# The first attention's routing of an eight-batch transformer kernel: nine pieces on VectorE, five roots on GpSimd, later output products

## The chip, the cores and the metric

The kernel runs on one core of one Trainium2 chip. The metric is the device time of one execution in microseconds; three runs of the kernel before gave 683.17, 691.25 and 2517.85, with a median of 691.25. A core has TensorE (PE: matmuls and transposes), VectorE (DVE), ScalarE (ACT), GpSimd (POOL) and SyncE (SP); they run their own instruction streams and wait for each other on semaphores. Sixteen DMA engines move data between HBM and the on-chip memories. TensorE's products land in PSUM, eight banks of 2 KB a partition.

## The reference

The input x has 8 batches of 128 rows by 256 columns, the context as many. Four residual blocks follow each other:

```python
x = x + cross_attention(layernorm(x), ctx)      # 16 heads over the 256 columns, rotary angles
x = x + moe(layernorm(x), 64 experts, top 8)    # softmax over the logits, gated expert MLPs
x = x + attention(layernorm(x), ctx)            # over the 128 rows, one head
x = x + moe(layernorm(x), 16 experts, top 4)

def cross_attention(query, key, value):         # per batch b and head h, d = 8
    scores = einsum('bdhn,bdhm->bhnm', rotary(q), rotary(k)) / sqrt(8)
    out = einsum('bhnm,bdhm->bdhn', softmax(scores), v)
    return einsum('oi,bin->bon', Wm, out) + bm
```

In the first expert block a row's logits, their eight largest and the softmax over them decide to which experts the row goes and with which weights. The change lies in the first block and in this routing, which is computed beside it.

## The kernel before, in words

The program has four phases. `project_phase` (0 to 64 us of the profile) makes queries, keys and values. `attend_phase` (to about 274 us) is the first attention together with the routing of the first expert block; all that changes lies in it. `held_phase` loads each expert's rows from HBM and runs the 64 experts; its first load of routed rows (`load_rows`, SyncE, L1174) waits until every scatter of the routing is done. `second_phase` holds the rest.

In `attend_phase` each engine runs a loop of its own over the same positions `at`. A position is a head: 16 a batch, 128 in all, from -20 (`LEAD`) to a little over 128. What an engine does at which position is written in its loop, and for the routing in a table, `RoutingSteps`: each stage has an offset, and batch b does it at position 16 b + offset. The order inside one position is the order of the loop's lines. Nothing is planned at run time: an engine that waits holds everything behind it.

A head goes through the engines in this way:
- **Maxima.** Twenty positions ahead TensorE makes the head's scores once (`score_for_top`, L926, two matmuls into one of two banks `ps_top`), and VectorE takes each row's maximum (`find_top`, L1021). TensorE may fill a bank only after the maximum of two heads before. After eight heads GpSimd cuts the maxima into three parts (`cut_tops`), TensorE transposes these (`turn_tops`, L934, bank `ps_rows`), ScalarE copies them (`keep_rows`), and SyncE writes them into rows of the queries (`place`), so that the scores come out with the maximum subtracted.
- **Scores and exponentials.** TensorE makes the scores again (`score`, L944, three banks `ps_score`); ScalarE takes the exponential (L1093) into a ring of twelve.
- **Output products.** For each group of four heads TensorE multiplies the exponentials with the values and a column of ones (`weigh`, L956, two halves, at positions 5 and 7 after the group's first head). After two groups, a pair of eight heads, ScalarE copies the pair's output out of PSUM (`keep_out`, L1077, position 8 p + 12 for pair p). For the second pair of batch b that is position 16 b + 20. In batches 0 to 3 ScalarE issues, right before that copy, the loads of the operands of batch b + 4.
- **The way through memory.** SyncE stores the pair to HBM (`store`, L860) and loads a batch's output and its sums packed into 128 partitions (`load_packed`, L869, two halves).

Then comes the routing of a batch, with its offsets in the table before (`AMID`, batches 0 to 4): load 26, share 34 (VectorE: a reciprocal, L1025, and the product with it, L1028), merge 37 (TensorE: Wm, L974), add 38 (VectorE: the residual, L1034, and the row statistics, L523 and L524), scale 39 (VectorE: the reciprocal root, ten short instructions, L532 to L538), norm 42 (ScalarE, L558), turn 46 (TensorE: two transposes), keep 47 (ScalarE, L607), score 51 (TensorE: the logits), choose 52 (VectorE: logits, the eight largest, the mask, L623 to L632), expo 55 (ScalarE), rank 55 (TensorE), places 57 and targets 59 (VectorE: the addresses), weights 62 (ScalarE, L665). From 62 on GpSimd scatters the batch's rows with eight indirect DMAs (L682). The last three batches have tables with smaller offsets.

`lift` is the merge's bias with the mean of the values' bias folded in: one small matmul (`lift_once`) after the inputs of the merge (`op_w`, `op_bias`, `op_gate`) have landed, and one VectorE addition. Right before it, at position -1, TensorE runs 24 warm-up matmuls (L991) whose results nobody reads. The bank `ps_merge` holds merge results, the transposed rows, logits and ranks in turn.

ScalarE also issues DMAs that clear the buffer of the routed rows (`act_empty`, 960 KB each, up to position 40), and ScalarE and SyncE load the first 32 experts' weights into memory that the attention frees: twelve early ones by ScalarE, twenty by SyncE behind its last packed load (L502).

## Time and profile before

| | us |
|---|---|
| runs shown | 683.17, 691.25, 2517.85 |
| their median | 691.25 |
| the profiled execution | 690.62 |
| its span | 688.9 |
| first attention, from the projections' end to its last instruction | 64 to 274 |
| first load of routed rows | 275.03 |

| engine | busy, share of the span |
|---|---|
| TensorE | 482.5 us, 70% |
| VectorE | 384.4 us, 56% |
| GpSimd | 349.4 us, 51% |
| ScalarE | 221.6 us, 32% |

Busy shares are averages over four phases with different limits. For a change inside one phase the timeline of that phase is read: at which time an engine issues the instruction that another waits for, and which wait ends last there. In a timeline row the first number is the start in us from the span's start, the second the duration, and the bracket behind the row the idle time before it with what ended it. TensorE's granted clock is 0.84 on the mean of the whole span; 1.0 is 2.4 GHz and 0.50 is 1.2 GHz.

### The profile page before, as it was taken

How to read it: one execution, taken by the hardware profiler on the slowest of the kernel's cores; microseconds unless marked ns; L12 is line 12 of the kernel's file. 1: busy time of each engine (PE TensorE's matmuls, PEld its weight loads, DVE VectorE, ACT ScalarE, POOL GpSimd, SP SyncE). 2: the span in 40 equal slices, each digit the busy share in tenths (PEclk: the TensorE clock that was granted, in tenths of full speed). 3: DMA queues.
4: the chain of work that ended last, by engine and by line, in shares of the span. 5: the costliest groups of instructions: out<-in, count | busy, mean ns of one | idle time of the engine just before them, and what ended most of it. 6: DMA issues, size and time to landing. Idle time of an engine off the chain costs nothing.

```text
span 688.9 us, 12080 instructions
## 1 busy us (share of the span) xinstructions
PE 482.5 (70%) x3519; PEld 368.4 (53%) x3519; DVE 384.4 (56%) x1235; ACT 221.6 (32%) x578; POOL 349.4 (51%) x476
## 2 busy tenths in 40 slices
PE   0741898888898430699989994157764499999960
PEld 0630344444443210688877783145553499999950
DVE  8981576788786460154444442689955044444426
ACT  0451065555667310333323331134431122222210
POOL 9394221115556673256545537014444867777730
PEclk9985599888899655799999998597765599999985
DMA  5089989746588697789999723961111799999927
GB/s 184 4 203 244 341 291 298 218 94 155 166 238 279 208 402 285 229 270 313 347 298 309 244 95 106 353 273 55 70 69 61 258 388 360 349 353 361 375 100 276
DMA packets 82915, 163.95 MB, mean 238 GB/s; under 512 B 13070, under 2 KB 58142, under 8 KB 81072
## 3 DMA queue, kind: packets, MB, share of 16 engines
q1 hardware_dynamic: 56832, 106.20, 46.3%
q0 software_dynamic: 13968, 32.29, 12.7%
q10 hardware_dynamic: 12064, 24.84, 12.4%
q8 instruction: 24, 0.39, 0.2%
q14 instruction: 27, 0.22, 0.1%
HBM read 104.94 MB, written 66.78 MB: 249 GB/s over the span
## 4 chain that ended last, share of the span: by engine, by line
PE 32%; DMA 13%; DVE 9%; issue 2%; POOL 2%; ACT 1%; SPq 1%; POOLq 0%; DVEq 0%
PE sc_ps L1790 11%; DMA hd_side<-held 6%; PE hd_ps_up L1246 6%; PE sc_ps L1772 5%; DMA rows<-hd_side_out,hd_side_target 3%; PE hd_ps_out L1252 2%; DMA sc_rows<-rows 2%; PE hd_ps_x L1224 2%; PE sc_ps L1780 1%; DVE sc_rows L1879 1%; PE sc_ps L1740 1%; POOL rows L1393 1%; PE sc_ps L1728 1%; DVE sc_n_stats L1473 1%; DMA listed<-sc_empty,sc_index 1%
## 5 line engine op out<-in xcount | busy, mean ns | idle before, releaser
L1021 DVE TENSOR_REDUCE at_top<-at_ps_top 128x2 f32<-128x512 f32 x128 | 83.2, 685 | 46.4 <-PE at_ps_top L926 45.6
L1393 POOL DMA_INDIRECT rows<-hd_out,hd_rows x64 | 62.2, 972 | 59.3 <-DVE hd_out L1344 36.9
L1093 ACT ACTIVATE at_prob<-at_ps_score 128x512 f32<-128x512 f32 x128 | 72.6, 594 | 51.2 <-PE at_ps_score L944 50.6
L926 PE MATMUL at_ps_top<-e_arena 96*128 96x256 bf16 x256 | 57.6, 315 | 37.2 <-PEq L107 21.9
L1246 PE MATMUL hd_ps_up<-hd_x_turned,e_arena 128*128 128x160 f32 x512 | 82.7, 305 | 0.0
L1790 PEld LDWEIGHTS sc_ps<-sc_t_turned,e_w 128*112 128x112 f32 x672 | 80.6, 180 | 2.6
L1790 PE MATMUL sc_ps<-sc_t_turned,e_w 128*112 128x128 f32 x672 | 82.0, 276 | 0.0
L1246 PEld LDWEIGHTS hd_ps_up<-hd_x_turned,e_arena 128*128 128x128 f32 x512 | 76.1, 192 | 8.7 <-issue 6.2
L682 POOL DMA_INDIRECT held<-e_extended,e_address x64 | 62.4, 975 | 28.4 <-issue 17.7
L682 POOL DMA_INDIRECT listed<-e_extended,e_address x32 | 33.6, 1049 | 69.0 <-DVE e_address L674 61.5
L1381 DVE TENSOR_TENSOR hd_inner<-hd_silu,hd_ps_up 128x160 f32<-128x160 f32 x64 | 20.5, 321 | 81.8 <-ACT hd_silu L1331 81.8
L944 PE MATMUL at_ps_score<-e_arena 99*128 99x256 bf16 x256 | 52.1, 293 | 3.2 <-DMA e_arena<-at_top_rows 3.2
L1686 POOL DMA_INDIRECT listed<-sc_empty,sc_index x48 | 46.8, 974 | 14.6 <-issue 12.5
L926 PEld LDWEIGHTS at_ps_top<-e_arena 96*128 96x128 bf16 x256 | 24.0, 107 | 55.3 <-DVE at_top L1021 28.3
L1691 POOL DMA_INDIRECT rows<-sc_out,sc_target x42 | 41.2, 981 | 22.2 <-POOL sc_index L1680 13.1
L956 PE MATMUL at_ps_out<-at_prob,e_arena 128*32 128x256 f32 x512 | 44.6, 423 | 5.4 <-ACT at_out L1077 4.5
L1331 ACT ACTIVATE hd_silu<-hd_ps_up 128x160 f32<-128x160 f32 x64 | 19.5, 304 | 82.4 <-PE hd_ps_up L1246 82.4
L1857 ACT ACTIVATE sc_silu<-sc_ps 112x256 f32<-112x256 f32 x42 | 16.1, 384 | 89.9 <-PE sc_ps L1790 89.9
L1772 PE MATMUL sc_ps<-e_w,sc_inner 112*128 112x256 f32 x168 | 43.3, 380 | 0.1
L899 POOL TENSOR_SCALAR at_top_cut<-at_top 128x16 bf16<-128x16 f32 x16 | 4.0, 252 | 73.0 <-DVE at_top L1021 73.0
L1344 DVE TENSOR_SCALAR hd_out<-hd_ps_out,hd_rows 128x256 f32<-128x256 f32 x64 | 30.9, 484 | 13.7 <-PE hd_ps_out L1252 12.0
L1252 PE MATMUL hd_ps_out<-e_arena,hd_inner 128*128 128x256 f32 x128 | 38.3, 381 | 0.3 <-DVE hd_inner L1381 0.3
(266 smaller groups left out, 911.6 us busy)
## 6 DMA issues: line engine op xcount, KB each, us to landing
e_w<-in_weights SPq DMA_DIRECT2D x42, 704.0 KB, 6.0
e_arena<-in_weights SPq DMA_DIRECT2D x52, 384.0 KB, 11.4
held<-e_empty ACTq DMA_DIRECT2D x16, 960.0 KB, 7.2
hd_rows<-held SPq DMA_DIRECT2D x15, 768.0 KB, 10.5
sc_rows<-rows SPq DMA_DIRECT2D x8, 1024.0 KB, 13.8
sc_tile_rows<-listed SPq DMA_DIRECT2D x42, 144.0 KB
parts<-op_parts SPq DMA_DIRECT2D x8, 576.0 KB, 6.7
e_arena<-in_weights ACTq DMA_DIRECT2D x12, 384.0 KB, 4.0
```

The lines of the kernel that those rows point to most:

```text
L682: self.nc.gpsimd.indirect_dma_start(self.held_dram, to, self.held.extended[:, b, :], None).then_inc(self.held.scattered, 16)
L926: last = nc.tensor.matmul(ps_top[at % TOPS][:, half, :], q_in[n][0:TOP, columns(at, half)], k_in[n][0:TOP, columns(at)], start=True, stop= ...
L944: last = nc.tensor.matmul(ps_score[at % SCORES][:, half, :], k_in[n][0:ROWS, columns(at, half)], q_in[n][0:ROWS, columns(at)], start=True, ...
L956: last = nc.tensor.matmul(ps_out[32 * j:32 * j + VW, g % 2, :], v_in[:, b, half, 4 * g + j, :], prob[(4 * group + j) % RING][:, half, :], ...
L1021: nc.vector.reduce_max(top[:, 2 * h:2 * h + 2], ps_top[at % TOPS][:], AX_X).then_inc(top_found, 1)
L1093: nc.scalar.activation(prob[at % RING][:], ps_score[at % SCORES][:], ACT.Exp, scale=scale).then_inc(prob_ready, 1)
L1246: op = nc.tensor.matmul(ps_up[e % 2][:, part, :], w[:, k, part * P:(part + 1) * P], x_turned[g % 2][:, j, k, :], start=k == 0, stop=k == 1)
L1252: nc.tensor.matmul(ps_out[e % 2][:], inner[e % INNERS][:, 0:P], ring.w[e % ring.SLOTS][:, 2, :], start=True, stop=True).then_inc(down_done, 1)
L1393: nc.gpsimd.indirect_dma_start(rows_out, to, out_ap, None, bounds_check=TOKENS * LAYER0.chosen - 1, oob_is_err=False).then_inc(semaphore, 16)
L1686: nc.gpsimd.indirect_dma_start(listed_dram, to, empty[:], None, bounds_check=E * TOKENS + 2 * U * P - 1, oob_is_err=False).then_inc(cleare ...
L1772: op = nc.tensor.matmul(ps_out[u % 2], inner[u % 2][:, c * P:(c + 1) * P], down_w[u][:, c, :], start=c == 0, stop=c == C - 1)
L1790: op = nc.tensor.matmul(ps_up[u % 2][:, part, c * P:(c + 1) * P], up_w[u][:, k, at:at + W], t_turned[u % 2][:, k, :], start=k == 0, stop=k ...
```

## The change

It moves stages, splits two of them and hands one to another engine; what is computed is the same, but that five roots are computed by a power in place of a first guess and Newton steps.

- Each batch has a table of its own. Of batches 0 to 3: load 25, invert0 30, invert1 31, share 32, merge 35, add 36, stats 37, scale 38, norm 41, turn 44, keep 45, score 49, best 50, mask 51, expo 53, rank 54, places 55, targets 57, weights 60. The scatters of a batch have a table (`SCATTERS`).
- VectorE's reciprocal is in two halves of 128 columns (`invert`), the choice in two pieces (`dve_best`, `dve_mask`), the statistics apart from the addition.
- The roots of batches 0 to 4 run on GpSimd (`pool_scale`, three instructions instead of ten), those of 5 to 7 stay on VectorE.
- The merge results move from the bank `ps_merge` to that of the transposed maxima (`ps_rows_merged`). The merge now waits for ScalarE's copy of these maxima and for the addition before, and some transposes wait for an addition.
- The two halves of the output products stand at 7, 9 and 10, 11 after a pair's first head, where they stood at 5, 7 and 9, 11.
- `lift_once` stands at position -2, ahead of the warm-up, and VectorE's addition at -1.

```diff
 class Rstd:
     def pool_scale(self, pool, link, b):
...
         link(nc.gpsimd.tensor_scalar(full, self.mean_var[:, 1:2], EPS, None, ALU.add))
         link(nc.gpsimd.tensor_tensor(root, full, self.power[:], ALU.pow))
-        for _ in range(NEWTON - 1):
...
 class RoutingSteps:
-    LOAD, SHARE = 26, 34
-    AMID = dict(load=LOAD, share=SHARE, merge=37, add=38, scale=39, norm=42, turn=46, keep=47, score=51, choose=52, expo=55, rank=55,
-                places=57, targets=59, weights=62, scatter=62)
-    LAST_BUT_TWO = dict(AMID, turn=45, keep=46, score=49, choose=49, expo=50, targets=50, rank=50, places=51, weights=51, scatter=53)
-    LAST_TWO = dict(load=LOAD, share=SHARE, merge=35, add=36, scale=37, norm=37, turn=39, keep=39, score=41, choose=41, expo=42, targets=42,
-                    rank=43, places=43, weights=43, scatter=46)
+    AMID = dict(load=25, invert0=30, invert1=31, share=32, merge=35, add=36, stats=37, scale=38, norm=41, turn=44, keep=45, score=49,
+                best=50, mask=51, expo=53, rank=54, places=55, targets=57, weights=60)
+    FOURTH = dict(AMID, score=48, best=49, mask=49, expo=51, rank=51, places=52, targets=53, weights=54)
+    FIFTH = dict(load=25, invert0=30, invert1=30, share=30, merge=34, add=34, stats=34, scale=34, norm=36, turn=39, keep=40, score=43,
+                 best=43, mask=43, expo=45, rank=44, places=45, targets=46, weights=47)
+    SIXTH = dict(load=25, invert0=30, invert1=30, share=30, merge=31, add=32, stats=32, scale=32, norm=33, turn=35, keep=35, score=37,
+                 best=37, mask=37, expo=38, rank=38, places=39, targets=39, weights=40)
+    SEVENTH = dict(load=25, invert0=34, invert1=34, share=34, merge=35, add=36, stats=36, scale=37, norm=37, turn=39, keep=39, score=41,
+                   best=41, mask=41, expo=42, rank=42, places=43, targets=43, weights=43)
+    BATCHES = (AMID, AMID, AMID, AMID, FOURTH, FIFTH, SIXTH, SEVENTH)
+    SCATTERS = ((60, 61, 62, 63, 68, 69, 71, 72),) * 3 + tuple(tuple(range(first, first + 8)) for first in (60, 54, 48, 43, 51))
+    BY_POOL = 5
...
 def attend_phase(...):
-        ps_rows = s.psum("ps_rows", [P, P])
+        ps_rows_merged = s.psum("ps_rows_merged", [P, 2 * D])
+        ps_rows, ps_merged = ps_rows_merged[:, 0:P], ps_rows_merged[:, D:]
         ps_merge = s.psum("ps_merge", [P, 2 * D])
-        ps_merged = ps_merge[:, 0:D]
...
+                b = steps("scale", at)
+                if b is not None and b < steps.BY_POOL:
+                    rstd.pool_scale(pool, link, b)
...
             def turn_tops(hh):
+                if hh == 1:
+                    pe.wait_ge(lift_known, 1)
+                if hh >= 6 and hh % 2 == 0:
+                    pe.wait_ge(x_ready, hh // 2 - 2)
...
             def lift_once():
                 pe.wait_ge(inputs.loaded, 48)
+                pe.wait_ge(rows_kept, 1)
...
             def merge(b):
-                if b >= B - 2:
-                    pe.wait_ge(routing.rank_read, b)
-                elif b >= 1:
-                    pe.wait_ge(routing.logits_read, b)
-                else:
-                    pe.wait_ge(lift_known, 1)
+                pe.wait_ge(rows_kept, min(2 * b + 6, HALVES))
+                if b >= 1:
+                    pe.wait_ge(x_ready, b)
                 pe.wait_ge(divided, b + 1)
...
-                if 4 <= at < B * H + 4 and at % 4 == 1:
-                    weigh(at // 4 - 1, 0)
-                if 4 <= at < B * H + 4 and at % 4 == 3:
-                    weigh(at // 4 - 1, 1)
+                for offset, late_group, half in ((7, 0, 0), (9, 0, 1), (10, 1, 0), (11, 1, 1)):
+                    p, late = divmod(at - offset, HALF)
+                    if late == 0 and 0 <= p < HALVES:
+                        weigh(2 * p + late_group, half)
...
+                if at == -2:
+                    lift_once()
                 if at == -1:
                     for _ in range(WARM_UP):
                         nc.tensor.matmul(ps_score[0][:, 0, :], k_in[0][0:TOP, 0:P], k_in[0][0:TOP, 0:D], start=True, stop=True)
-                    lift_once()
...
                 if b is not None:
-                    if b + 1 < B - 2:
-                        pe.wait_ge(x_ready, b + 2)
                     routing.pe_rank(pe, b)
...
+            def invert(b, half):
+                if half == 0:
+                    dve.wait_ge(packed_loaded[b % 2], 32 * (b // 2 + 1))
+                link.free(nc.vector.reciprocal(share[:, half * P:(half + 1) * P], packed[b % 2][:, 1, half * P:(half + 1) * P]))
+
             def divide(b):
-                dve.wait_ge(packed_loaded[b % 2], 32 * (b // 2 + 1))
-                link(nc.vector.reciprocal(share[:], packed[b % 2][:, 1, :]))
+                dve.wait_ge(link.semaphore, link.count)
...
-                if at == 0:
+                if at == -1:
                     dve.wait_ge(lift_ready, 1)
```

The first place is VectorE's stream over one batch of the middle. `at_top` are the maxima of one head each, `at_share` the reciprocal, `at_heads` the output that the merge takes, `at_r_logits` to `e_mask` the choice of another batch's experts, `x_all` the residual. Before:

```order
L1021 TENSOR_REDUCE at_top<-at_ps_top 128x2 x7
L1025 RECIPROCAL at_share<-at_packed 128x256
L1028 TENSOR_TENSOR at_heads<-at_packed,at_share 128x256
L1021 TENSOR_REDUCE at_top<-at_ps_top 128x2 x2
L623 COPY at_r_logits<-at_ps_merge 128x64
L627 MAX at_r_best<-at_r_logits 128x8
L628 TENSOR_SCALAR at_r_minus_top<-at_r_best 128x1
L631 MATCH_REPLACE at_r_taken<-at_r_best,at_r_logits 128x64
L632 TENSOR_SCALAR e_mask<-at_r_taken 128x64
L1021 TENSOR_REDUCE at_top<-at_ps_top 128x2 x2
L1034 SCALAR_TENSOR_TENSOR x_all<-at_ps_merge,at_lift,x_all 128x256
```

And after:

```order
L1030 TENSOR_REDUCE at_top<-at_ps_top 128x2 x5
L1035 RECIPROCAL at_share<-at_packed 128x128
L1030 TENSOR_REDUCE at_top<-at_ps_top 128x2
L1035 RECIPROCAL at_share<-at_packed 128x128
L1030 TENSOR_REDUCE at_top<-at_ps_top 128x2
L1041 TENSOR_TENSOR at_heads<-at_packed,at_share 128x256
L1030 TENSOR_REDUCE at_top<-at_ps_top 128x2 x2
L623 COPY at_r_logits<-at_ps_merge 128x64
L627 MAX at_r_best<-at_r_logits 128x8
L628 TENSOR_SCALAR at_r_minus_top<-at_r_best 128x1
L1030 TENSOR_REDUCE at_top<-at_ps_top 128x2
L634 MATCH_REPLACE at_r_taken<-at_r_best,at_r_logits 128x64
```

Reciprocal, product and choice, each whole between two maxima before, stand in pieces between single maxima, and the reciprocal four heads earlier; the ten instructions of the root, which followed the statistics, are gone from the stream of batches 0 to 4.

The second place is TensorE's stream just ahead of the first head. `at_ps_top` are the products for the maxima, `at_ps_rows` the transposed maxima, `op_bias,op_w` the merge's inputs in `lift_once`, the 24 products of L991 (after: L1003) the warm-up, and L944 (after: L956) the first scores. Before:

```order
L926 MATMUL at_ps_top<-e_arena 128x256 x24
L934 MATMUL at_ps_rows<-identity,at_top_parts 48x128
L926 MATMUL at_ps_top<-e_arena 128x256 x16
L934 MATMUL at_ps_rows<-identity,at_top_parts 48x128
L991 MATMUL at_ps_score<-e_arena 128x256 x24
L964 MATMUL at_ps_merge<-op_bias,op_w 128x1
L944 MATMUL at_ps_score<-e_arena 128x256 x2
```

And after:

```order
L934 MATMUL at_ps_top<-e_arena 128x256 x24
L946 MATMUL at_ps_rows_merged<-identity,at_top_parts 48x128
L934 MATMUL at_ps_top<-e_arena 128x256 x14
L977 MATMUL at_ps_rows_merged<-op_bias,op_w 128x1
L934 MATMUL at_ps_top<-e_arena 128x256 x2
L946 MATMUL at_ps_rows_merged<-identity,at_top_parts 48x128
L1003 MATMUL at_ps_score<-e_arena 128x256 x24
L956 MATMUL at_ps_score<-e_arena 128x256 x2
```

The small product of `lift_once`, which stood behind the warm-up, now stands ahead of the last head's products for its maxima, of the second transpose and of the warm-up.

The third place is ScalarE's stream around its last copy of a pair's output (`at_out`). `at_r_turned_sb` is the copy of a batch's transposed rows, `e_extended` with `at_n_scale` its normalisation and with `at_r_share` its weights. Before:

```order
L607 ACTIVATE at_r_turned_sb<-at_ps_merge 128x256
L665 ACTIVATE e_extended<-at_r_expo,at_r_share 128x64
L1093 ACTIVATE at_prob<-at_ps_score 128x512
L638 ACTIVATE at_r_expo,at_r_total<-at_r_logits,at_r_minus_top 128x64
L665 ACTIVATE e_extended<-at_r_expo,at_r_share 128x64
L1077 ACTIVATE at_out<-at_ps_out 128x512
L558 ACTIVATE e_extended<-x_all,at_n_scale 128x256
L607 ACTIVATE at_r_turned_sb<-at_ps_merge 128x256
```

And after:

```order
L641 ACTIVATE at_r_expo,at_r_total<-at_r_logits,at_r_minus_top 128x64
L1118 ACTIVATE at_prob<-at_ps_score 128x512 x2
L668 ACTIVATE e_extended<-at_r_expo,at_r_share 128x64
L554 ACTIVATE e_extended<-x_all,at_n_scale 128x256
L603 ACTIVATE at_r_turned_sb<-at_ps_merge 128x256
L1102 ACTIVATE at_out<-at_ps_out 128x512
L641 ACTIVATE at_r_expo,at_r_total<-at_r_logits,at_r_minus_top 128x64
L668 ACTIVATE e_extended<-at_r_expo,at_r_share 128x64
```

Batch 6's normalisation and copy, which followed the last copy of a pair's output, now stand ahead of it.

## Rows read from the trace of the kernel before

**Rows 1.** Waits of TensorE, 105 to 226: us in total, times, longest us

```profile
PE at_ps_top L926 <- DVE at_top L1021: 13.1, 13, 2.2
```

**Rows 2.** Timeline of VectorE, batch 2: start us, us, instruction [idle before]

```profile
159.43 1.74 DVE L1025 RECIPROCAL at_share<-at_packed 128x256 f32<-128x256 f32 x1
...
166.61 0.14 DVE L532 TENSOR_SCALAR at_n_work<-at_n_mean_var 128x1 f32<-128x1 f32 x1
...
168.46 1.28 DVE L1021 TENSOR_REDUCE at_top<-at_ps_top 128x2 f32<-128x512 f32 x2
```

**Rows 3.** Timeline of ScalarE, output copies, batches 0 to 3 and 5, the end

```profile
105.29 0.60 ACT L1077 ACTIVATE at_out<-at_ps_out 128x512 f32<-128x512 f32 x1 [3.01 <-issue]
...
122.67 0.60 ACT L1077 ACTIVATE at_out<-at_ps_out 128x512 f32<-128x512 f32 x1 [3.42 <-issue]
...
140.81 0.60 ACT L1077 ACTIVATE at_out<-at_ps_out 128x512 f32<-128x512 f32 x1 [1.79 <-issue]
...
161.50 0.60 ACT L1077 ACTIVATE at_out<-at_ps_out 128x512 f32<-128x512 f32 x1 [1.81 <-issue]
...
199.20 0.60 ACT L1077 ACTIVATE at_out<-at_ps_out 128x512 f32<-128x512 f32 x1 [0.17 <-PE at_ps_out L956]
...
231.64 0.58 ACT L1077 ACTIVATE at_out<-at_ps_out 128x512 f32<-128x512 f32 x1
...
237.40 0.38 ACT L607 ACTIVATE at_r_turned_sb<-at_ps_merge 128x256 f32<-128x256 f32 x1 [0.84 <-PE at_ps_merge L601]
```

**Rows 4.** Timeline of SyncE's queue: start, us of issuing, transfer

```profile
76.76 1.13 SPq L445 DMA_DIRECT2D op_gate<-in_gate  x1
...
113.56 1.95 SPq L869 DMA_DIRECT2D at_packed<-attended  x2
...
131.27 1.56 SPq L869 DMA_DIRECT2D at_packed<-attended  x2
...
162.12 0.37 SPq L860 DMA_DIRECT2D attended<-at_out  x1
...
171.05 1.19 SPq L869 DMA_DIRECT2D at_packed<-attended  x2
...
222.29 1.20 SPq L869 DMA_DIRECT2D at_packed<-attended  x2
...
235.69 18.79 SPq L502 DMA_DIRECT2D e_arena<-in_weights  x20
...
275.03 0.34 SPq L1174 DMA_DIRECT2D hd_rows<-held  x1
```

**Rows 5.** Timeline of VectorE, batch 0

```profile
119.47 1.75 DVE L1025 RECIPROCAL at_share<-at_packed 128x256 f32<-128x256 f32 x1 [0.40 <-DMA at_packed<-attended]
```

**Rows 6.** Timeline of VectorE, the last two batches

```profile
230.61 0.42 DVE L1028 TENSOR_TENSOR at_heads<-at_packed,at_share 128x256 f32<-128x256 f32 x1
...
242.81 0.42 DVE L1028 TENSOR_TENSOR at_heads<-at_packed,at_share 128x256 f32<-128x256 f32 x1
...
252.83 0.17 DVE L674 CAST e_address<-at_r_highest 128x8 int32<-128x8 f32 x1
```

**Rows 7.** Timeline of GpSimd, the last scatter

```profile
266.17 0.96 POOL L682 DMA_INDIRECT held<-e_extended,e_address  x1 [0.30 <-issue]
```

**Rows 8.** Windows: from:to, us, each engine's busy (x), PEclk, DMA share, GB/s

```profile
268.00:270.00 2.00, 0.00 (x0) 0.00 (x0) 0.00 (x0) 0.00 (x0) 0.00 (x0) 0.50 1.04 420
```

**Rows 9.** Timeline of TensorE, warm-up and first scores

```profile
79.22 5.03 PE L991 MATMUL at_ps_score<-e_arena 96*128 96x256 bf16 x24
85.28 0.39 PE L944 MATMUL at_ps_score<-e_arena 99*128 99x256 bf16 x2 [0.92 <-DMA e_arena<-at_top_rows]
```

**Rows 10.** DMA issues, 70 to 86: transfer, queue, count, KB, median us to landing

```profile
e_arena<-at_top_rows SPq DMA_DIRECT2D x3, 4.0 KB, 5.3
```

**Rows 11.** The tile of the packed outputs, over the whole span

```profile
DMA to landing us min/median/max: 2.5/3.0/4.0
```

**Rows 12.** Windows, the stretch after the root of batch 2

```profile
172.00:174.00 2.00, 2.00 (x16) 0.96 (x13) 1.16 (x2) 1.45 (x3) 1.27 (x6) 0.50 0.68 201
```

More of the change, by code:

```diff
@@ L543, in pool_scale @@
     def pool_scale(self, pool, link, b):
-        nc, (full, square, work) = self.nc, (self.work[:, k:k + 1] for k in range(3))
+        nc, full = self.nc, self.work[:, 0:1]
         root, shift = self.scale[:, b % 2, 0:1], self.scale[:, b % 2, 1:2]
@@ L549, in pool_scale @@
         link(nc.gpsimd.tensor_tensor(root, full, self.power[:], ALU.pow))
-        for _ in range(NEWTON - 1):
-            link(nc.gpsimd.tensor_tensor(square, root, root, ALU.mult))
-            link(nc.gpsimd.tensor_scalar(work, square, full, -0.5, ALU.mult, ALU.mult))
-            link(nc.gpsimd.tensor_scalar(root, work, 1.5, root, ALU.add, ALU.mult))
         nc.gpsimd.tensor_scalar(shift, self.mean_var[:, 0:1], root, -1.0, ALU.mult, ALU.mult).then_inc(self.ready, 1)
@@ L616, in dve_choose, with dve_best @@
     def dve_choose(self, dve, link, b):
+        self.dve_best(dve, link, b)
+        self.dve_mask(dve, link, b)
+    def dve_best(self, dve, link, b):
         nc, E = self.nc, self.layer.experts
@@ L628, in dve_choose, with dve_mask @@
         nc.vector.tensor_scalar(self.minus_top[:], self.best[:, 0:1], -1.0, None, ALU.mult).then_inc(self.top_known, 1)
+    def dve_mask(self, dve, link, b):
+        nc, E = self.nc, self.layer.experts
         if self.spare:
@@ L763, in __init__ @@
+    SEVENTH = dict(load=25, invert0=34, invert1=34, share=34, merge=35, add=36, stats=36, scale=37, norm=37, turn=39, keep=39, score=41,
[3 more added lines that the diff above has]
+    BY_POOL = 5
     def __init__(self):
-        of_batch = [self.AMID] * (B - 3) + [self.LAST_BUT_TWO] + [self.LAST_TWO] * 2
@@ L765, in __init__ @@
-        self.batch = {}
-        for b, offsets in enumerate(of_batch):
-            for stage, offset in offsets.items():
+        self.batch, self.scatters = {}, {}
+        for b in range(B):
+            for stage, offset in self.BATCHES[b].items():
                 self.batch[stage, b * H + offset] = b
+            for k, offset in enumerate(self.SCATTERS[b]):
+                self.scatters.setdefault(b * H + offset, []).append((b, k))
         self.end = max(at for _, at in self.batch) + 1
-        self.scatters = {}
@@ L771, in __init__ @@
-        for b, offsets in enumerate(of_batch):
-            first = b * H + offsets["scatter"]
-            apart = H // 2 if first < B * H - H - 4 else LAYER0.chosen // 2
-            for k in range(LAYER0.chosen):
-                self.scatters.setdefault(first + k % 4 + k // 4 * apart, []).append((b, k))
         self.first_scatter = min(self.scatters)
@@ L907, in _ @@
             operands.set_rows(nc, pool, DEEP - 1)
+            rstd.pool_start(link)
             for at in range(-LEAD, END + LEAD):
@@ L1035, in add, with stats @@
                                                ALU.add, ALU.add).then_inc(x_ready, 1)
+            def stats(b):
                 dve.wait_ge(x_ready, b + 1)
@@ L1041, in _ @@
                     find_top(at + LEAD)
-                if at == 0:
+                if at == -1:
                     dve.wait_ge(lift_ready, 1)
                     nc.vector.tensor_tensor(lift[:], ps_merged[:, 0:1], inputs.bias[:, 1:2], ALU.add).then_inc(lift_known, 1)
+                b = steps("best", at)
+                if b is not None:
+                    routing.dve_best(dve, link, b)
+                b = steps("mask", at)
+                if b is not None:
+                    routing.dve_mask(dve, link, b)
+                for half in range(2):
+                    b = steps(f"invert{half}", at)
+                    if b is not None:
+                        invert(b, half)
                 b = steps("share", at)
@@ L1050, in _ @@
                     add(b)
+                b = steps("stats", at)
+                if b is not None:
+                    stats(b)
                 b = steps("scale", at)
-                if b is not None:
+                if b is not None and b >= steps.BY_POOL:
                     rstd.dve_scale(dve, link, b)
-                b = steps("choose", at)
-                if b is not None:
-                    routing.dve_choose(dve, link, b)
                 b = steps("targets", at)
```

## The prediction, made before the changed kernel was run

> **What bounds the kernel now.** I read the chain of waits first. Its first long step is SyncE's load of routed rows at 275.03 [rows 4]; from there to the end nothing that the change touches runs. So the change moves the end by as much as it moves this load, and the sum is made on it. Then I read TensorE's waits inside the attention: 13.1 us in 13 waits are for VectorE's maxima [rows 1]. VectorE's timeline shows why: the reciprocal (1.74) and the root (from 166.61 to the next maximum at 168.46, 1.85) stand whole between two maxima [rows 2]. Then the rows of the way through memory: ScalarE's copy of a pair's output, SyncE's store, its load of the packed outputs [rows 3, 4], VectorE's reciprocal behind it [rows 5]. Last the tail: VectorE's last batches, GpSimd's last scatter, the DMA engines [rows 6 to 8].
>
> I write K0 to K5 for the copies at positions 20, 36, ... of the head loop: 105.29, 122.67, 140.81, 161.50 and, for K5, 199.20 [rows 3]. The profiled execution took 690.62 us, 0.6 under the median of 691.25.
>
> **The start: +4.0.** lift_once moves from behind the warm-up to position -2, and waits for all three merge inputs. The last, the gate, is issued at 76.76 [rows 4]. Its landing isn't shown; the transfers issued next to it took 5.3 [rows 10], the shortest packed load 2.5 [rows 11], the longest visible one 5.9 (113.56 [rows 4] to 119.47 [rows 5]). I take 5.3, the neighbours' value: TensorE waits until 82.1, where before it went on and began the warm-up at 79.22 [rows 9]. Behind the wait stand one more top product, its maximum (0.64, half of the pair in [rows 2]), the lift's addition, for which the second transpose now waits, and that transpose: an estimate of 2.1. The 24 warm-up matmuls begin at 84.2 instead of 79.22, 5.0 later; the first score had waited 0.92 for a DMA after them [rows 9], so the heads begin 4.0 later. With 2.5 it is +1.2, with 5.9 +4.6.
>
> **The batches: -1.0.** The reciprocal moves from position 34 to 30 and 31, in halves; the packed load moves by one position only, and SyncE passes nothing with it, since its neighbours there stand at 24 and 28. So VectorE comes four heads earlier to data that come no earlier, and its wait holds the maxima behind it, and so TensorE.
> When does VectorE reach position 30? Batch 2 took 18.6 us from its copy to the reciprocal (140.81 to 159.43), 14 heads; ten are 13.3, less the root of 1.85, which goes to GpSimd: 11.4. In batch 0, without a root, ten of 14 heads make 9.8 (13.8 without the wait of 0.40, [rows 3, 5]).
> When has the load landed? Batch 0: 119.47, K0 + 14.2. Batch 1: issued at 131.27, the second half 0.6 later, landing 3.0 (median, [rows 11]): 134.9, K1 + 12.2. Batch 3: its store was issued at 162.12 and the load could go only at 171.05 [rows 4], so K3 + 13.2. In these batches the operand load that ScalarE issues just before the copy (idle 3.01, 3.42, 1.81 by issue, [rows 3]) fills the DMA engines together with the clearing of the row buffer or with scatters. Batch 2 has the operand load but neither of the others, batch 4 none of it; I take both as landed in time.
> From position 30 to the next copy: four maxima (2.56), two halves (1.75), the product (0.42, [rows 6]) make 4.7, and then what lies today between the start of a reciprocal and the next copy: 3.2 in batch 0 (119.47 to 122.67), 2.1 in batch 2 (159.43 to 161.50); without an operand load to issue (1.8) 0.3.
> - Batch 0: 14.2 + 4.7 + 3.2 = 22.1 against 17.4: +4.7.
> - Batch 1: 12.2 + 4.7 + 2.1 = 19.0 against 18.1: +0.9.
> - Batch 2: 11.4 + 4.7 + 2.1 = 18.2 against 20.7: -2.5.
> - Batches 3 and 4: 13.2 + 4.7 + 0.3 = 18.2 and 11.4 + 4.7 + 0.3 = 16.4, together 34.6 against 37.7 (161.50 to 199.20): -3.1.
> - Batch 4's root leaves the stretch after K5, where maxima are needed for eight more heads only: half of 1.85, -0.9 (ends 0 and -1.85).
> The sum is -0.9, which I round to -1.0. The splits of logits and mask, and of addition and statistics, remove no work; they are in these numbers as shorter holds. The output products of a pair begin two heads later: TensorE no longer stands behind the copy that operand issue delays, but in batches 0, 1 and 3 the landing sets the pace anyway, so I price it at nothing (at most the 3.4 that ScalarE is late).
> GpSimd's five roots are three instructions each. A power on it is in no row; the ends are 0 (hidden) and, by its dearest row, a scatter of 0.96 [rows 7], about 3 us a batch. Behind two scatters at positions 36 and 37 it is due before ScalarE's position 41: hidden, I take 0; its cover gone, ScalarE's normalisation waits and the scores behind it.
>
> **The tail: -2.0,** on top of the shift so far. Batch 6's packed load (222.29, landed 225.9) is now used at once: product done at 228.1 instead of 231.0 [rows 6], so -2.9 for that batch. But ScalarE's normalisation and copy of batch 6 now stand ahead of the last output copy. The turned copy ended at 237.78 [rows 3]; less 2.9 it ends at 234.9, so the output copy ends at 235.5 instead of 232.2: +3.3. Its store and load and then the weights on SyncE (235.69, [rows 4]) go with it. The last packed load, landed by 238.1 today (0.6 before the weights, plus 3.0), comes at 241.4, plus 2.2 for reciprocal and product 243.6, where today the product ends at 243.2: batch 7 gains nothing (+0.4). Its addresses are ready at 253.4, eight scatters of 1.26 end at 263.5, against 267.13 today, where GpSimd runs without a gap: -3.6.
> The other end: the DMA engines are full until 270 [rows 8]. The weights start 3.3 later, while eight scatters (0.2 MB each at 0.42 MB per us, 3.7 us) have gone ahead: -0.4. The gate lies 7.9 behind the last scatter and 5 behind the end of traffic; which of them sets it the trace doesn't say. Between -3.6 and -0.4 I take the middle, -2.0.
>
> **Sum:** 4.0 - 1.0 - 2.0 = +1.0, and 690.62 becomes **691.6**: no change, within what 2% (13.8 us) can tell.
>
> **Rivals.**
> A, the loads land in time everywhere. For it speaks that packed loads land in 3.0 where the engines are free; against it three batches of four. Batch 0 would gain nothing (9.8 + 4.7 + 3.2 = 17.7, +0.3), batch 1 18.2 (+0.1), batches 3 and 4 32.8 (-4.9): -7.9 with the rest, total 684.7. If VectorE alone sets the pace, position 30 comes at 9.5 (ten maxima, 3.1 of other pieces), 1.9 less in four batches: 677. I say 681.
> The Trainium skill's page "DMA: Bandwidth & Descriptors", section "Anatomy of one DMA", prices a transfer at a fixed 2.0 us plus bytes over 436 GB/s, for GpSimd's path; by it the store of 256 KB would be an estimate of 2.6 and each load of 128 KB 2.3, and the result would be this rival's. The 3.0 agrees; the 8.9 of batch 3 doesn't.
> B, the waits bring TensorE's clock down, and it ends slower than before. While it waits for data, TensorE does nothing. Today windows at 0.50 follow its waits, as 172 to 174, where it was busy throughout [rows 12]; 170 to 176 reads the same. Such a stretch of 6 us costs up to 3. It decides if the stretches at 1.2 GHz grow in number with the waits of batches 0, 1 and 3: 9 us, and 0.6 for the start at its upper end: 701.
> The page "TensorE: Matmul & The Clock Gate" of the Trainium skill, section "HAM oscillation", describes a kernel that falls back to the low clock in each tile because of its DMA wait; that would be this rival.
> C, the roots don't leave the path: GpSimd is late behind its scatters, ScalarE waits at position 41. In batches 2 to 4, 2 us each: 697.6.
>
> **How the numbers follow.** Forecast 0.55 (686 to 697: start 1.2 to 4.6, tail -3.6 to -0.4, batches 3 either way), A 0.25, B 0.13, C 0.07. The range from 678 to 701 leaves out the fastest of A and the slowest of B. Faster by over 2% (under 677.4) only if A holds with VectorE's pace and a short start: 0.10. Slower by over 2% (above 705) needs B with more stretches than counted: 0.05. Within: 0.85.
>
> **What would show it.** The warm-up begins near 84 behind a wait in front of the lift; else the start is wrong. VectorE idles before the first half reciprocal until the packed load, some 4 us in batch 0, under 2 in the others; no idle means A. TensorE's waits for maxima outside these fall well below 13.1. ScalarE's last output copy stands behind batch 6's turned copy; GpSimd idles before batch 7's scatters. The prediction is wrong if the load of routed rows moves by more than 10 us.

## The result and the profile after

The changed kernel took 702.91 us (median of four runs, 701.74 to 704.54) beside 690.95 of the kernel before (683.17, 690.65, 691.25 and 2517.85). Over the fast runs alone, that is without the 2517.85, it takes 1.0228 times as long, 95% interval 1.0178 to 1.0277; the two medians as they stand give 1.0173. It is slower, and whether by more than 2% the interval leaves open. It lies 1.9 us outside the stated range, and near the 701 of rival B.

The span of the profiled execution grew from 688.9 to 700.6, by 11.7. By stretches, from the same rows of both traces:

| stretch | before | after | moved by | forecast |
|---|---|---|---|---|
| to the first score | 85.28 | 90.59 | +5.3 | +4.0 |
| first score to K0 | 20.0 | 21.1 | +1.1 | 0 |
| K0 to K1 | 17.4 | 23.6 | +6.2 | +4.7 |
| K1 to K2 | 18.1 | 19.9 | +1.7 | +0.9 |
| K2 to K3 | 20.7 | 20.0 | -0.7 | -2.5 |
| K3 to K5 | 37.7 | 39.4 | +1.7 | -3.1 |
| K5 to batch 6's copy (position 116) | 16.5 | 16.8 | +0.2 | -0.9 |
| from there to the load of routed rows | 59.3 | 58.2 | -1.1 | -2.0 |
| from there to the end | 413.9 | 411.2 | -2.7 | 0 |

The last stretch isn't touched; over the runs of this study it lay between 410.6 and 415.4, whatever the kernel.

TensorE's timeline at the start, after (columns as in [rows 9]):

```profile
83.33 0.59 PE L977 MATMUL at_ps_rows_merged<-op_bias,op_w 128*128 128x1 f32 x2 [5.06 <-DMA op_gate<-in_gate]
...
85.47 5.33 PE L1003 MATMUL at_ps_score<-e_arena 96*128 96x256 bf16 x24
90.59 0.63 PE L956 MATMUL at_ps_score<-e_arena 99*128 99x256 bf16 x2
```

The wait of 5.06 for the gate stands where it was forecast, ahead of the lift; the gate landed 1.2 later than the 82.1 taken.

VectorE's waits from 111 to 240 (the sixth is batch 5's), then the first half reciprocal of batches 0 to 4 in its timeline, after:

```profile
DVE at_share L1035 <- DMA at_packed<-attended: 14.9, 6, 4.5
```

```profile
125.68 0.95 DVE L1035 RECIPROCAL at_share<-at_packed 128x128 f32<-128x128 f32 x1 [2.51 <-DMA at_packed<-attended]
...
146.71 0.95 DVE L1035 RECIPROCAL at_share<-at_packed 128x128 f32<-128x128 f32 x1 [2.66 <-DMA at_packed<-attended]
...
165.37 0.95 DVE L1035 RECIPROCAL at_share<-at_packed 128x128 f32<-128x128 f32 x1 [1.47 <-DMA at_packed<-attended]
...
185.70 0.95 DVE L1035 RECIPROCAL at_share<-at_packed 128x128 f32<-128x128 f32 x1 [1.73 <-DMA at_packed<-attended]
...
206.34 0.95 DVE L1035 RECIPROCAL at_share<-at_packed 128x128 f32<-128x128 f32 x1 [2.01 <-DMA at_packed<-attended]
```

VectorE waits for the packed load in each of these batches, where before it waited 0.40 in batch 0 [rows 5] and not at all in 1 to 4. TensorE's waits for maxima over the same stretch, its wait in batch 2, and windows around it (last three columns: granted clock, DMA share, GB/s):

```profile
PE at_ps_top L934 <- DVE at_top L1030: 10.9, 7, 2.8
```

```profile
166.93 0.61 PE L934 MATMUL at_ps_top<-e_arena 96*128 96x256 bf16 x2 [1.72 <-DVE at_top L1030]
```

```profile
164.00:166.00 2.00, 1.21 (x15) 0.61 (x7) 0.63 (x1) 1.69 (x5) 1.35 (x2) 1.00 0.65 204
166.00:168.00 2.00, 1.07 (x10) 0.33 (x10) 2.00 (x4) 0.04 (x1) 1.70 (x2) 0.73 0.50 180
168.00:170.00 2.00, 2.00 (x15) 1.37 (x8) 1.19 (x3) 0.00 (x0) 1.12 (x2) 0.50 0.34 124
170.00:172.00 2.00, 2.00 (x14) 0.64 (x12) 1.20 (x4) 0.60 (x1) 0.00 (x0) 0.50 0.30 104
172.00:174.00 2.00, 2.00 (x12) 0.77 (x11) 1.08 (x4) 0.60 (x1) 0.60 (x3) 0.56 0.00 0
174.00:176.00 2.00, 1.82 (x17) 1.21 (x14) 1.28 (x3) 0.88 (x2) 1.52 (x6) 1.00 0.98 213
```

The total of these waits fell from 13.1 [rows 1] to 10.9, and there are seven in place of 13. But TensorE, at 1.00 ahead of the wait, comes out of it at 0.50, and is busy throughout three windows with 15, 14 and 12 matmuls (in fill, below, such windows hold 24 and 25 at 1.00). The same happens behind the waits of batches 0, 1, 3 and 4 (2.76, 1.65, 1.98 and 2.26 us): in each of the five the clock then is at 0.50 for some 3 to 7 us. Before, half clock came too, behind some of the roots and reciprocals. From K0 to batch 6's copy, before and after (us, then the engines' busy times, TensorE's first):

```profile
105.29:215.72 110.43, 95.41 (x809) 48.47 (x809) 86.80 (x207) 67.44 (x142) 43.12 (x103) 0.88 0.71 198
```

```profile
111.68:231.24 119.56, 100.76 (x816) 48.26 (x817) 79.58 (x170) 65.71 (x144) 51.96 (x121) 0.84 0.66 191
```

Of the 9.1 that this stretch grew, TensorE was busy for 5.4 more, with about as many matmuls at a lower clock, and idle for 3.8 more.

The copies K1 to K5, ScalarE's timeline, and its last copy with what stands ahead of it (in [rows 3] the order is the other way round):

```profile
135.29 0.60 ACT L1102 ACTIVATE at_out<-at_ps_out 128x512 f32<-128x512 f32 x1 [3.28 <-issue]
...
155.15 0.60 ACT L1102 ACTIVATE at_out<-at_ps_out 128x512 f32<-128x512 f32 x1 [2.45 <-issue]
...
175.12 0.60 ACT L1102 ACTIVATE at_out<-at_ps_out 128x512 f32<-128x512 f32 x1 [2.49 <-issue]
...
193.73 0.60 ACT L1102 ACTIVATE at_out<-at_ps_out 128x512 f32<-128x512 f32 x1 [0.87 <-PE at_ps_out L968]
...
214.48 0.60 ACT L1102 ACTIVATE at_out<-at_ps_out 128x512 f32<-128x512 f32 x1 [0.87 <-PE at_ps_out L968]
...
249.57 0.38 ACT L603 ACTIVATE at_r_turned_sb<-at_ps_merge 128x256 f32<-128x256 f32 x1 [0.84 <-PE at_ps_merge L597]
249.85 0.59 ACT L1102 ACTIVATE at_out<-at_ps_out 128x512 f32<-128x512 f32 x1
```

GpSimd's first scatter of batch 7 and SyncE's load of routed rows, after:

```profile
270.24 0.95 POOL L685 DMA_INDIRECT held<-e_extended,e_address  x1 [4.18 <-DVE e_address L677]
```

```profile
289.42 0.33 SPq L1199 DMA_DIRECT2D hd_rows<-held  x1
```

GpSimd, without a gap before [rows 7], now idles 4.18 ahead of batch 7's scatters, as forecast.

### The profile page after: what moved, and what is told of

It reads as the page before. It is cut to its first block, busy times and chain, and to the rows that moved or that the text cites. A ratio compares the mean times of both kernels' runs of the same rounds, so it can differ in the third digit from the quotient of the medians.

```text
span 700.6 us, 12050 instructions
## 1 busy us (share of the span) xinstructions
PE 492.5 (70%) x3519; PEld 369.2 (53%) x3519; DVE 376.3 (54%) x1193; ACT 220.0 (31%) x578; POOL 355.7 (51%) x492
## 4 chain that ended last, share of the span: by engine, by line
PE 31%; DMA 12%; DVE 10%; issue 2%; POOL 1%; ACT 1%; SPq 0%; POOLq 0%; DVEq 0%; ACTq 0%
PE sc_ps L1815 11%; DMA hd_side<-held 6%; PE hd_ps_up L1271 6%; PE sc_ps L1797 5%; DMA rows<-hd_side_out,hd_side_target 3%; PE hd_ps_out L1277 2%; PE hd_ps_x L1249 2%; DMA sc_rows<-rows 2%; PE sc_ps L1805 1%; DVE sc_rows L1904 1%; PE sc_ps L1753 1%; POOL rows L1418 1%; DVE sc_n_stats L1498 1%; PE hd_ps_side L1283 1%; PE sc_ps L1765 1%
## 5 line engine op out<-in xcount | busy, mean ns | idle before, releaser
L1418 POOL DMA_INDIRECT rows<-hd_out,hd_rows x64 | 62.2, 972 | 58.8 <-DVE hd_out L1369 36.2
L956 PE MATMUL at_ps_score<-e_arena 99*128 99x256 bf16 x256 | 52.6, 293 | 7.7 <-ACT at_prob L1118 5.1
L1711 POOL DMA_INDIRECT listed<-sc_empty,sc_index x48 | 46.8, 974 | 14.9 <-issue 12.6
L968 PE MATMUL at_ps_out<-at_prob,e_arena 128*32 128x256 f32 x512 | 49.3, 467 | 0.0
L1882 ACT ACTIVATE sc_silu<-sc_ps 112x256 f32<-112x256 f32 x42 | 16.1, 384 | 89.4 <-PE sc_ps L1815 89.4
L956 PEld LDWEIGHTS at_ps_score<-e_arena 99*128 99x128 bf16 x256 | 22.4, 104 | 30.2 <-ACT at_prob L1118 20.4
## 6 DMA issues: line engine op xcount, KB each, us to landing
e_arena<-in_weights SPq DMA_DIRECT2D x52, 384.0 KB, 11.2
sc_rows<-rows SPq DMA_DIRECT2D x8, 1024.0 KB, 13.2
```

Source lines behind the costliest of these rows:

```text
L956: last = nc.tensor.matmul(ps_score[at % SCORES][:, half, :], k_in[n][0:ROWS, columns(at, half)], q_in[n][0:ROWS, columns(at)], start=True, ...
L968: last = nc.tensor.matmul(ps_out[32 * j:32 * j + VW, g % 2, :], v_in[:, b, half, 4 * g + j, :], prob[(4 * group + j) % RING][:, half, :], ...
L1418: nc.gpsimd.indirect_dma_start(rows_out, to, out_ap, None, bounds_check=TOKENS * LAYER0.chosen - 1, oob_is_err=False).then_inc(semaphore, 16)
L1711: nc.gpsimd.indirect_dma_start(listed_dram, to, empty[:], None, bounds_check=E * TOKENS + 2 * U * P - 1, oob_is_err=False).then_inc(cleare ...
```

## The experiments

Each was timed beside the kernel before on the same chip (688.0 to 689.3 there), and its ratio is to that. The changed kernel is the 702.91 above. The kernel before itself has medians from 688.0 to 691.0 in these timings, so a difference between two runs in us is good to some 3 us, and the ratios compare better. Rows, waits and stretches are of one execution each.

**fill: the wait or the clock?** TensorE gets work for the time of VectorE's wait.

```diff
+                if at % H == 1 and 2 * H < at < 7 * H:
+                    pe.wait_ge(prob_ready, at - SCORES + 2)
+                    ... # 16 matmuls into ps_score[(at + 1) % SCORES]
                 if at + LEAD < B * H:
                     score_for_top(at + LEAD)
```

> The changed kernel, with 16 matmuls whose results nobody reads put where TensorE waits in batches 0 to 4 (position 33). VectorE's wait for the packed load stays. Theory 1 (the wait lets TensorE's clock fall to 1.2 GHz for some 6 us in each batch, and that costs more than the wait): the granted clock stays at 1.00 behind the waits and the time falls by 5 to 9 us, to 694 to 698. Theory 2 (the wait alone costs, the clock is a side effect that the slack of the other engines hides): no change, 702 to 705, even where the clock stays up. Theory 3 (the later output products hold the heads up): no change either.

Measured: 700.21, ratio to before 1.018 (1.0126 to 1.0235). Batch 2 in TensorE's timeline and in windows:

```profile
163.20 1.91 PE L993 MATMUL at_ps_score<-e_arena 96*128 96x256 bf16 x16
165.69 0.39 PE L934 MATMUL at_ps_top<-e_arena 96*128 96x256 bf16 x2 [0.58 <-DVE at_top L1035]
```

```profile
164.00:166.00 2.00, 1.42 (x13) 0.86 (x10) 1.86 (x3) 0.19 (x1) 1.66 (x2) 1.00 0.50 182
166.00:168.00 2.00, 2.00 (x25) 1.11 (x24) 2.00 (x5) 0.50 (x1) 1.24 (x2) 1.00 0.36 129
168.00:170.00 2.00, 2.00 (x24) 1.02 (x17) 1.90 (x8) 0.69 (x2) 0.17 (x1) 1.00 0.26 98
```

In batches 1 to 3 the clock stays up behind waits of VectorE that are longer than in the changed kernel (3.18, 2.08 and 2.10, against 2.66, 1.47 and 1.73), and the stretch from the reciprocal to the next copy takes 6.9, 6.9 and 5.3 (19.1) where the changed kernel takes 8.4, 9.8 and 8.0 (26.2). In batches 0 and 4 the clock fell all the same (windows at 0.50 from 130 and from 204). There the filler did not cover the wait: TensorE still stood idle for 2.12 and 1.85 us, in batches 1 to 3 for 0.71, 0.58 and 0.30:

```profile
126.98 0.39 PE L934 MATMUL at_ps_top<-e_arena 96*128 96x256 bf16 x2 [2.12 <-DVE at_top L1035]
...
202.74 0.39 PE L934 MATMUL at_ps_top<-e_arena 96*128 96x256 bf16 x2 [1.85 <-DVE at_top L1035]
```

From K1 to K4, which is batches 1 to 3, it takes 52.7 where the changed kernel takes 58.4: of the 7.1 us that the clock gave, 1.4 went into longer waits for the load. The total moved by 2.7, less than theory 1 gave, and the two intervals overlap, so what the clock is worth is read from the trace alone: the load of routed rows comes at 283.64, 5.8 earlier, though batch 4's packed load came later (wait 3.70), while the untouched stretch behind it took 414.8, 3.6 more.

**late: the reciprocal back behind its data.**

```diff
-    AMID = dict(load=25, invert0=30, invert1=31, share=32, merge=35, add=36, stats=37, ...
+    AMID = dict(load=25, invert0=33, invert1=34, share=34, merge=36, add=37, stats=37, ...
```

> The changed kernel with the reciprocal's halves and the product of batches 0 to 4 back at positions 33, 34 and 34 (from 30, 31 and 32), merge at 36, add and statistics at 37. All else of the change stays. Theory 1 and 2 (the reciprocal comes to its data before they land): VectorE's wait for the packed load goes under 0.5 us a batch, the batches lose 7 to 10 us, 693 to 696. Theory 3 (the later output products, or GpSimd's roots, hold the heads up): within 2 us of the changed kernel, 701 to 705.

Measured: 685.04, ratio 0.996 (0.9939 to 0.9981): 18 under the changed kernel, twice what was expected. Batches 1 and 2 on VectorE and batch 2's wait on TensorE:

```profile
144.46 0.94 DVE L1035 RECIPROCAL at_share<-at_packed 128x128 f32<-128x128 f32 x1
...
160.53 0.94 DVE L1035 RECIPROCAL at_share<-at_packed 128x128 f32<-128x128 f32 x1
```

```profile
165.63 0.39 PE L934 MATMUL at_ps_top<-e_arena 96*128 96x256 bf16 x2 [0.20 <-DVE at_top L1030]
```

No wait for the load in batches 1 to 4 and no window at half clock from 136 to 224. K2 to K3 takes 16.1, K3 to K4 15.1. K0 to K5 takes 84.0, in the changed kernel 102.8, before 93.9: the difference lies in these batches. K1 to K4 takes 49.7: of the 8.7 under the changed kernel's 58.4, fill brought 5.7 with the clock alone. From K0 to batch 6's copy (the view of the result's section, for late):

```profile
112.49:212.99 100.50, 89.54 (x816) 44.45 (x817) 79.81 (x171) 66.42 (x145) 50.51 (x119) 0.95 0.76 221
```

Here are 816 matmuls as in the changed kernel, at 0.95 in place of 0.84: of the 19.1 us less, 11.2 are TensorE's busy time and 7.8 its idle time.

**early_before: the move of the reciprocal alone, on the kernel before.**

```diff
-    AMID = dict(load=LOAD, share=SHARE, merge=37, ...
+    AMID = dict(load=LOAD, share=30, merge=37, ...
```

> The kernel before with one move alone: the whole reciprocal and its product at position 30 in place of 34, batches 0 to 5. Roots, output products and lift as before. Theory 1: VectorE waits some 2 us for the packed load in each batch, the clock falls behind each wait, 6 to 10 us slower than before, 697 to 701. Theory 3: at most 2 us slower. If VectorE with its own root comes late enough, the wait is under 1 us and the time is unchanged: then the move hurts only together with the roots on GpSimd.

Measured: 698.4, ratio 1.0132 (1.0089 to 1.0176). The size is theory 1's, its place is not. VectorE, batches 0 and 1:

```profile
120.96 1.75 DVE L1025 RECIPROCAL at_share<-at_packed 128x256 f32<-128x256 f32 x1 [2.54 <-DMA at_packed<-attended]
...
143.78 1.74 DVE L1025 RECIPROCAL at_share<-at_packed 128x256 f32<-128x256 f32 x1
```

Only batch 0 waits (K0 to K1 23.9, +6.5); batches 1 to 4, where VectorE still does the roots, show no wait, and K1 to K5 together take 0.5 more than before. The first score came 1.2 later and the untouched last stretch took 1.5 more, which is part of the 10. Nor does before_roots, below, wait in batches 0 to 4. So neither move alone puts a wait into each batch, and the change, which has both, has one in each: the roots' leaving brings VectorE to position 30 ahead of its data. The two moves alone on the kernel before, without the rest of the change, were not run.

**lift: the start.**

```diff
-                if at == -2:
+                if at == 2:
                     lift_once()
```

(VectorE's addition at 3; the third transpose waits for it in place of the second.)

> The changed kernel with the lift's small product at position 2, behind the warm-up, and its addition at 3. The first score comes at 85 to 86 in place of 90.6. If the start adds to the batches as the sum has it, the time falls by 5 us, to 697 to 699. If the batches then only wait longer for their loads, by 1 to 2 us.

Measured: 698.36, ratio 1.0165 (1.0133 to 1.0198), 4.5 less, as the sum has it. Batch 0's first score comes at 86.4, 4.2 earlier.

**late_lift: both.**

> Both at once: the reciprocal back at 33 and 34 (685.0 alone) and the lift behind the warm-up (4.5 less than the changed kernel alone). If the two add, 679 to 682. If batch 0, which then starts 5 us earlier, only waits longer for its packed load (2.7 us with the late reciprocal alone), 683 to 685.

Measured: 680.77, ratio 0.9877 (0.9824 to 0.993). They add.

**late_lift_op: operand loads behind the packed load.**

```diff
-                b = batch_at(at, H + 4)
+                b = batch_at(at, 26)
```

> The same two, and ScalarE's operand loads of batches 4 to 7 issued at position 26, behind the packed load's issue, in place of 20, ahead of the copy of the pair's output. Theory (these loads fill the DMA engines ahead of the store and of the packed load, and hold the copy up): batch 0's wait falls by 2 us or more, the copies are not held up by their issue, and the time is 2 to 5 us under that of the two alone. Rival (the packed load's way is as long without them): within 1 us of it.

Measured: 688.39, ratio 0.9996 (0.9965 to 1.0028): 7.6 slower than the two alone. In its profiled execution (683.35, the fastest of ten) the copy K0 comes at 102.05 in place of 108.24, but TensorE now waits 9.4 us in five waits for the rows of maxima that SyncE writes (late_lift: 2.5). The traffic was moved onto another transfer; what it does to the packed load this run can't say.

**late_roots and late_whole: what the other parts are worth.** `BY_POOL = 0` and `invert0=34, invert1=34, share=34`, each on late.

> The reciprocal back at 33 and 34, and all roots back on VectorE. If VectorE sets the pace once its wait is gone, the root's 1.85 comes back in five batches, as a hold of TensorE with a fall of the clock behind it: 8 to 14 us over the 685.0 of the late reciprocal alone. If it lies beside other work, at most 2 us over it.

> The reciprocal at 34 in one piece with the product, between two maxima; the roots on GpSimd. If the splitting into heads of their own keeps TensorE's waits short and with that its clock up, one hold of 2.2 us a batch brings the half clock back in batches 1 to 4: 5 to 10 us over the 685.0 of the halves. If only the removal of the root counts, within 2 us of it.

Measured: late_roots 695.5, ratio 1.01 (1.0068 to 1.0133), 10.5 over late; TensorE's waits for maxima go from 3.8 to 11.5 us, and stretches at half clock come back at 172 and 210, behind two of the four waits of 1.83 to 1.87 that the roots make in batches 1 to 4. So here the price of the roots is the waits first and the clock in part: from K0 to batch 6's copy it takes 8.6 more than late, of which TensorE is idle for 6.4 and busy for 2.2. late_whole 688.0, ratio 1.0014 (0.9978 to 1.0049), 3 over late, short of the 5 expected: batches 1 to 4 keep the clock and take 66.4 as in late, and K5 to batch 6's copy takes 21.2 in place of 16.5 behind a wait of 5.6 for batch 5's packed load.

**before_roots: the roots alone, on the kernel before.**

```diff
-                if b is not None:
+                if b is not None and b >= 5:
                     rstd.dve_scale(dve, link, b)
```

(and the three instructions in GpSimd's loop, as in the change.)

> The kernel before with one part of the change alone: the roots of batches 0 to 4 on GpSimd, three instructions each. Going by the late reciprocal, where the roots were worth 10 us, 6 to 10 us faster than before, 679 to 683, with fewer stretches at half clock. If the whole reciprocal, which stays between two maxima, keeps TensorE's waits and the low clock, at most 3 us faster. If GpSimd is late behind its scatters, slower than before.

Measured: 681.81, ratio 0.9889 (0.985 to 0.9927), 7.5 faster. TensorE's waits for maxima fall from 13.1 to 7.3.

**late_lift_weigh: the output products.** Offsets 5, 7, 9, 11 again, on late_lift.

> The faster version (late reciprocal, lift behind the warm-up) with the output products back at 5, 7, 9 and 11. The prediction priced their move at nothing: within 2 us of 680.8. If they leave heads for the copy out of PSUM, TensorE waits for ScalarE's copy where its issue of operand loads holds it, up to 3 us in batches 0 to 3: 685 to 692.

Measured: 682.19, ratio 0.9883 (0.9844 to 0.9921), within 2 of late_lift. Their move is worth nothing that can be measured. What it moves is the wait: in batch 0 TensorE waits 2.81 for ScalarE's copy here, and 2.23 in late_lift and after for an exponential that stands behind the same copy in ScalarE's stream.

**tail: batch 6 behind the last copy.**

```diff
-    SIXTH = dict(..., scale=32, norm=33, turn=35, keep=35, score=37, best=37, mask=37, expo=38, rank=38, places=39, targets=39, weights=40)
+    SIXTH = dict(..., scale=32, norm=36, turn=37, keep=37, score=39, best=39, mask=39, expo=40, rank=40, places=41, targets=41, weights=42)
```

> The faster version with batch 6's normalisation and turned copy behind the last copy of a pair's output, as before the change (norm 36, turn and keep 37, and what follows). The last copy comes 3 to 4 us earlier against batch 6's, and with it the last packed load and batch 7's addresses. If the last scatters set the load of routed rows, 2 to 3 us less than 680.8; if the DMA engines' traffic sets it, within 1 us.

Measured: 676.54, ratio 0.9809 (0.9765 to 0.9853): 4.2 under late_lift and the fastest version of the study. Its last copy and load of routed rows:

```profile
223.69 0.60 ACT L1102 ACTIVATE at_out<-at_ps_out 128x512 f32<-128x512 f32 x1 [2.31 <-PE at_ps_out L968]
```

```profile
263.32 0.33 SPq L1199 DMA_DIRECT2D hd_rows<-held  x1
```

Against batch 6's copy (207.74; late_lift 208.61) the last copy comes 1.2 earlier, not 3 to 4, and the load of routed rows 1.9; the rest of the 4.2 isn't seen in these rows. The two profiled executions lie only 2.0 apart (676.43 and 678.40, the fastest of late_lift's four), and the intervals of the two ratios overlap, so the 4.2 is not clear of noise.

**weights_later: what makes batch 4's load late.**

```diff
-        for at in range((DEEP + 1) * H + 4, B * H - 8, 3):
+        for at in range((DEEP + 2) * H, B * H - 8, 2):
```

> The changed kernel with ScalarE's twelve early loads of expert weights at positions 96, 98, ... 118 in place of 84, 87, ... 117: none is issued before batch 4's packed load has been used at position 94. If these loads make batch 4's packed load late (issued at 200.90, used at 206.34, VectorE waiting 2.01), the wait falls under 0.5 and batch 4 gets 2 to 4 us shorter (20.8 before); batch 5's packed load may then be later, since the loads stand closer together. If they don't, the wait stays at 2.

Measured: 704.47, ratio 1.0196 (1.0115 to 1.0278). SyncE's load, VectorE and TensorE in batch 4:

```profile
204.71 1.21 SPq L873 DMA_DIRECT2D at_packed<-attended  x2
```

```profile
208.49 0.95 DVE L1035 RECIPROCAL at_share<-at_packed 128x128 f32<-128x128 f32 x1 [0.48 <-DMA at_packed<-attended]
```

```profile
210.04 0.39 PE L934 MATMUL at_ps_top<-e_arena 96*128 96x256 bf16 x2 [0.73 <-DVE at_top L1030]
```

The load, issued at 204.71, is used 3.8 later (5.4 in the changed kernel), and the batch takes 17.0 in place of 20.8; with the weights in their place and the reciprocal at 30, VectorE waited 2.01 (after), 3.70 (fill) and 3.48 (lift). So it was the expert weights that made this load late. No half clock follows in batch 4, and from the reciprocal to the copy it takes 5.3 in place of 8.1, where the forecast's term gives 5.0. The total doesn't show it: in this execution batches 0 and 1 were 2.4 longer, with a wait of 4.90 in batch 0, which lies ahead of the edit; that wait was 2.51 (after), 3.62 (fill) and 4.92 (lift) in the other runs with the reciprocal at 30. The untouched last stretch took 2.0 more.

## Why the prediction was wrong

The step that failed is the batches: -1.0 was forecast, +10.2 came, first score to batch 6's copy. By the prediction's own sign, too, it was wrong: the load of routed rows moved by 14.4, more than the 10 it allows.

- **The term that was mis-sized** is the one from the start of the reciprocal to the next copy: "four maxima (2.56), two halves (1.75), the product (0.42) make 4.7, and then what lies today between the start of a reciprocal and the next copy". Over batches 0 to 4 it gives 7.9 + 6.8 + 6.8 + 5.0 + 5.0 = 31.5. Measured, from the rows above: 9.6 + 8.4 + 9.8 + 8.0 + 8.1, together 44.0 before rounding. The sum lets TensorE run at its pace of today behind a wait; it ran at half clock there. This is shown by fill for batches 1 to 3 (with the clock kept up 19.1, where the term gives 18.6) and by weights_later for batch 4 (5.3, and 5.0); for batch 0 (9.6, and 7.9) no run kept the clock up, and it is argued from the others.
- **When the data land** was not the miss. From each copy to its reciprocal the forecast has 14.2, 12.2, 11.4, 13.2 and 11.4, together 62.4; measured 14.0, 11.4, 10.2, 10.6 and 12.6, together 58.8, which is 3.6 less. With the term's 12.5 more that makes 8.9 of the 11.2 by which the batches missed; the rest is about 1.1 ahead of K0 and 1.1 behind K5. What was wrong is that batches 2 and 4 would not wait: VectorE came to position 30 before 11.4, and batch 4's load was late by the expert weights, which the argument on "none of it" left out.
- **Rival B** is what happened, at 701 and 0.13. Its mechanism stood in the text, its price was left out of the sum although [rows 12] showed it. That its 701 lies so near is in part luck: it counts 9 us for three new stretches at half clock, where five came and those of before behind the roots went, and TensorE's busy time grew by 5.4 and its idle time by 3.8. Half clock followed the wait in each of batches 0 to 4. The Trainium skill's page "TensorE: Matmul & The Clock Gate", section "HAM oscillation", tells of a kernel that falls back to the low clock in each tile by its DMA wait. The trace agrees in this, though the page's kernel has longer waits than TensorE's 1.65 to 2.76 here. Rival A is refuted by the waits. Rival C is refuted too: on GpSimd the three instructions of a root took 1.3 (136.24 to 137.50 in batch 0), and ScalarE waits for none of the five.
- **The start** was right in mechanism and 1.3 short: the gate landed 6.8 after its issue, not 5.3. lift gives 4.2 of the 5.3 back.
- **The tail** was right in mechanism: the last copy behind batch 6's, GpSimd idle; it gave -1.1 where -2.0 was taken. tail puts the price of that order at 1.9 by the traces; the 4.2 of the medians is not clear of noise.
- **The roots** were under-priced, as 1.85 off VectorE's way: 7.5 alone, 10.5 on late (9.6 by the ratios). On VectorE they hold TensorE, and a hold costs the wait and the clock behind it. Without them the stretch from K0 to batch 6's copy is 6.9 shorter on the kernel before, of which 5.7 are TensorE's busy time, and 8.6 shorter on late, of which 2.2 are. In the change this gain was lost, since VectorE only came earlier to a wait.
- **The splits** were priced as nothing of their own; late_whole bounds the reciprocal's by 3 to 4, none of it in batches 1 to 4; those of the choice and of the statistics were not run alone.

So two parts of the change work against each other: the roots' move brings VectorE forward, and the reciprocal's move takes that room and four heads more, which the packed load doesn't have.

What stays open: how much of batches 0 to 3's late loads is the operand loads' traffic, why the heads ahead of K0 took 1.1 longer, and what, besides a wait's length, decides whether half clock follows it.

## What to carry to other kernels

Before a stage is moved forward, subtract the landing of its data from the time at which its engine will come to it, after all other parts of the change have been counted; where that is negative, the wait stands in an in-order stream and holds everything behind it. Price such a wait as its length and, if TensorE stands behind it, half of the stretch of 1.2 GHz that the trace shows behind waits like it, which is an estimate from above. When a change of several parts is slower, undo the one that waits first: here a reciprocal put back by three heads turned 702.9 into 685.0, and with the lift's and batch 6's order put back the rest of the change is worth 1.9%, of which the roots alone give 1.1%.

## What was not expected of the hardware

- A wait of TensorE of 1.65 to 1.98 us was followed by some 3 to 7 us at 1.2 GHz (batches 1 to 3 after), waits of 0.58 (fill, batch 2) and 0.73 (weights_later, batch 4) by none. It is not a rule of the wait's length: of late_roots' four waits of 1.83 to 1.87 two were followed by none.
- The three instructions of a root on GpSimd took 1.3 us, the power among them, 128 by 1, 0.57, where VectorE's ten instructions for the same root took 1.85 [rows 2]:

```profile
136.55 0.57 POOL L549 TENSOR_TENSOR at_n_scale<-at_n_work,at_n_power 128x1 f32<-128x1 f32 x1
```
